# Two steps moved and one PSUM bank exchanged in a one-core transformer block with graph attention

## What is computed

```python
# layer 0, 16 heads of 16
x_mod = rms(x) * (1 + scale_msa) + shift_msa
q, k, v = split(x_mod @ qkv_w)                 # q, k: rms per head, rope
x = x + gate_msa * (softmax(q k^T / 4) v @ proj_w + proj_b)
h = rms(x) * (1 + scale_mlp) + shift_mlp
x = x + gate_mlp * ((silu(h @ w1) * (h @ w3)) @ w2)       # hidden width 704
# layer 1, 16 heads, keys are the first 20 tokens of a sequence
self_feat = concat(x, cond) @ W_self.T + b_self
for d in (0, 1):                               # two directions of the adjacency, 11 labels
    cond_adj, label_bias = A.sum(-1), A @ w_bias + b_bias
    aff = where(cond_adj > 0, (self_feat Wq) (kv Wk)^T / 4, NEG) + label_bias
    output += softmax(aff) kv Wout + bout
return x + relu(output)
```

## Time and profile before

| what | value |
| --- | --- |
| runs | 1407.96, 1402.92, 1408.21 us |
| the profiled execution | 1400.84 us, its span 1398.9 us |
| PE busy | 1334.7 us, 95% of the span |
| weight loads (PEld) busy | 1228.6 us, 88% |
| DVE busy | 1161.8 us, 83% |
| ACT busy | 888.6 us, 64% |
| POOL busy | 719.1 us, 51% |
| mean granted TensorE clock | 0.977 of full |
| time of one pass | 40.97 us (702.16 to 743.13, start of the same step on PE) |

### The profile page before, as it was taken

One profiled execution on the slowest core, in us unless ns is written; L12 is line 12 of the kernel. 1 busy time (PEld: TensorE's weight loads), 2 busy tenths in 40 slices (PEclk: granted clock), 3 DMA queues, 4 the chain that ended last, 5 costly groups with the idle time before them and its releaser, 6 DMA issues. The chain is left out here.

```text
span 1398.9 us, 51521 instructions
## 1 busy us (share of the span) xinstructions
PE 1334.7 (95%) x20276; PEld 1228.6 (88%) x20276; DVE 1161.8 (83%) x2065; ACT 888.6 (64%) x1784; POOL 719.1 (51%) x676
## 2 busy tenths in 40 slices
PE   4589999999999999999999999999999999999986
PEld 3579999999999999999999999999999999999875
DVE  5669888888888888888988888898888888888753
ACT  4557666666766666676666667666667667666542
POOL 0245655555565555456555546555555655555441
PEclk9689999999999999999999999999999999999997
DMA  7001111100011110011111001111100111110100
GB/s 243 29 24 31 46 43 43 43 28 25 33 43 43 43 43 18 33 35 43 43 43 43 15 32 39 43 43 43 43 15 28 43 43 43 43 43 8 30 22 9
DMA packets 49827, 56.19 MB, mean 40 GB/s; under 512 B 4352, under 2 KB 47744, under 8 KB 49792
## 3 DMA queue, kind: packets, MB, share of 16 engines
q1 hardware_dynamic: 48944, 53.86, 12.3%
q10 hardware_dynamic: 848, 1.84, 0.4%
HBM read 47.03 MB, written 8.65 MB: 40 GB/s over the span
## 5 line engine op out<-in xcount | busy, mean ns | idle before, releaser
L1318 POOL TENSOR_TENSOR gl<-gf,gh 128x512 fp32r<-128x512 f32 x96 | 124.2, 1294 | 261.6 <-ACT gh L926 261.6
L486 PE MATMUL psum<-nh,w_lo 128*128 128x256 f32 x704 | 182.7, 289 | 0.0
L486 PE MATMUL psum<-nh,w_hi 128*128 128x256 f32 x704 | 177.7, 284 | 0.0
L1318 POOL TENSOR_TENSOR nl<-xn,nh 128x512 fp32r<-128x512 f32 x64 | 98.3, 1536 | 123.2 <-ACT nh L864 123.2
L486 PEld LDWEIGHTS psum<-nh,w_lo 128*128 128x128 f32 x704 | 133.9, 190 | 0.2 <-issue 0.2
L486 PEld LDWEIGHTS psum<-nh,w_hi 128*128 128x128 f32 x704 | 133.2, 189 | 0.0
L1384 POOL TENSOR_TENSOR e<-e,inv 128x640 f32<-128x640 f32 x64 | 82.0, 1282 | 89.2 <-DVE inv L1274 89.2
L486 PE MATMUL psum<-nl,w_hi 128*128 128x256 f32 x704 | 115.5, 282 | 0.0
L926 ACT ACTIVATE gh<-gf 128x512 fp32r<-128x512 f32 x96 | 60.3, 628 | 61.7 <-DVE gf L1202 60.9
L486 PEld LDWEIGHTS psum<-nl,w_hi 128*128 128x128 f32 x704 | 98.0, 188 | 0.0
L486 PE MATMUL psum<-qkv_lo,nh 128*128 128x512 f32 (+1 forms) x256 | 87.8, 354 | 2.8 <-ACT nh L864 2.8
(11 more groups left out here) (186 smaller groups left out, 4414.0 us busy)
## 6 DMA issues: line engine op xcount, KB each, us to landing
adj<-in_adj SPq DMA_DIRECT2D x32, 440.0 KB, 3.4
x_in<-in_x SPq DMA_DIRECT2D x32, 256.0 KB, 2.7
xn<-in_xT SPq DMA_DIRECT2D x32, 256.0 KB, 3.5
x_res<-in_xT SPq DMA_DIRECT2D x32, 256.0 KB, 3.6
out_T<-y SPq DMA_DIRECT2D x32, 256.0 KB, 2.2
e<-in_adaln ACTq DMA_DIRECT2D x2, 512.0 KB, 5.2
stage<-in_qkv SPq DMA_DIRECT2D x2, 384.0 KB, 5.6
pT<-in_w SPq DMA_DIRECT2D x2, 384.0 KB, 7.1
```

The costliest lines, as they stand in the source:

```text
L486: last = nc.tensor.matmul(out, lhsT, rhs, start=start and i == 0, stop=stop and i == len(terms) - 1)
L1318: return nc.gpsimd.tensor_tensor(out, full, hi.bitcast(F32), ALU.subtract)
```

## The change

ACT's list has `self_split` directly behind `self`, ahead of `norm1_mean` and `keys`. DVE's list has `edges` ahead of the second `mix`; it stood behind `mix1`. The second half of tile 1's transposed probabilities goes to bank 7 and no longer to bank 0, and the waits for free banks follow from that. No instruction is added or taken out.

```diff
-    ..., "probsT": (5, 4, 4, 0), ...
+    ..., "probsT": (5, 4, 4, 7), ...
 DVE:
-        (1, "mlp_up", 1), (2, "mix", 1), (3, "qkv", 0), (3, "qkv", 1), (1, "mlp_up", 2), (0, "mix1", 0),
-        (1, "edges", 0), (3, "rope_scale", 0), (0, "out", 0),
+        (1, "mlp_up", 1), (1, "edges", 0), (2, "mix", 1), (3, "qkv", 0), (3, "qkv", 1), (1, "mlp_up", 2), (0, "mix1", 0),
+        (3, "rope_scale", 0), (0, "out", 0),
 Activation:
-        (2, "heads", 0), (2, "heads", 1), (0, "self", 0), (1, "norm1_mean", 0), (0, "keys", 0), (0, "self_split", 0),
+        (2, "heads", 0), (2, "heads", 1), (0, "self", 0), (0, "self_split", 0), (1, "norm1_mean", 0), (0, "keys", 0),
 PE, qkv, t == 0:
-                    wait_free(pe, m, (v1_kept, -3, 1), (normed[1], -2, 1), (qkT_kept, -1, 1))
+                    wait_free(pe, m, (pT_b, -1, 2))
 PE, score:
-                wait_free(pe, m, (g_done, -2, 3), (pT_b, -1, 2))
+                wait_free(pe, m, (g_done, -2, 3), (shifted_s, -1, 2))
 PE, probs_t, (t, j) == (1, 4):
-                        wait_free(pe, m, (biased1, -2, 4), (shifted_s, 0, 2))
+                        wait_free(pe, m, (v1_kept, -2, 1), (normed[1], -1, 1), (qkT_kept, 0, 1))
 PE, mlp_up, (2, "w3"):
-                        wait_free(pe, m, (pT1_a, -1, 1), (pT_b, 1, 2))
+                        wait_free(pe, m, (pT1_a, -1, 1), (biased1, -1, 4), (shifted_s, 1, 2))
 PE, probs_t1, (t, j) == (0, 0):
-                        wait_free(pe, m, (pT_b, 2, 2), (biased1, 0, 4))
+                        wait_free(pe, m, (biased1, 0, 4))
```

More of the change, by code:

```diff
@@ L72 @@
 BANK = {
-    "xT": 6, "qk": (2, 3), "v": (7, 1), "heads": (7, 5), "probsT": (5, 4, 4, 0), "probsT1": (0, 5, 4, 7),
+    "xT": 6, "qk": (2, 3), "v": (7, 1), "heads": (7, 5), "probsT": (5, 4, 4, 7), "probsT1": (0, 5, 4, 7),
     "mix": (5, 6), "q1": (4, 6), "score": 0, "score1": 0, "mixT": 6, "proj": 2, "norm1": 7, "up": (6, 4, 6),
```

## The result

The changed kernel takes 1390.09 us (median of four, 1388.06 to 1393.36) against 1406.68 us for the kernel before (four runs, 1402.92 to 1408.21). The ratio is 0.9893, 95% interval 0.9870 to 0.9916: faster by 1.1%, 16.6 us between the medians. The prediction said 1391.8, or 16.2 us less.

A forecast was written before the change was run, and what follows sets the result against it. The order of PE's own work was taken to set the time; closing two holes, 10.3 and 6.5 us, less a 0.6 us leftover wait, gave 16.2 off the 1407.96 median: 1391.8 us, range 1385 to 1409.

The forecast's parts named there:

- The bound: PE is busy 40.87 of 41.00 us a pass; two small holes of outside cause cost 0.56 a pass, 16.8 us.
- Self split first: ACT's high part of self_feat earlier: PE's 0.33 wait for POOL's low part goes, 10.3 us, L1086 taking 0.42.
- The first rival: POOL's power holds DVE's L1086, so the 0.33 hole moves to tile 0's transposition; 6.5 to 9.2 us gained; chance 0.20.
- The bank: Fifth transposition of tile 1's probabilities no longer waits for DVE's last bias (L1251): 0.23 x 28 = 6.5 us.
- Edges earlier: DVE's count fits its 1.37 us idle before the second mix; `y` eats the 0.97 freed; costed at zero.
- The sum: -10.3 - 6.5 + 0.6 = -16.2 us, giving 1391.8 us from the median; this forecast's chance 0.52.
- The third rival: POOL's L1368 holds DVE's count, delaying the second mix: PE loses 1.2 us a pass, 34 in all, 1442; chance 0.10 with other losses.
- The second rival: PE's holes return whole at other waits with 0.1 to 0.3 us to spare; time stays at 1408; chance 0.18.

## Why the prediction was right

*The bound.* PE's stream, with two holes of outside cause. Right: with both closed, the pass fell by 0.54 of the 0.56.

*Self split first, 10.3 us.* Right in mechanism, and nearly in size: alone it gives 0.31 a pass, 8.7 us in the loop's 28 passes; the 10.3 counted 31 waits of 0.33. The hole's 0.33 is kept because L1086 comes free, as argued; the version with one scaling moved shows that a later L1086 costs PE what it loses. (L1233 was called a fifth of L1086's size; with 80 of 256 columns it is about a third, which the argument doesn't need.) The first rival rested on POOL's power holding L1086. The trace after has just that overlap in the pass shown, and L1086 at 415 ns in the median of all passes. The Trainium skill, page "SBUF — State Buffer", section "Who interferes with whom", has the two exclude each other for the whole instruction; for the full-size operations that nearly holds here (L1086 before the change ends 0.29 behind POOL's operation, L1131's pair 0.61, `y` 0.54; but with an overlap of 0.21 L1086 lost only 0.07), for the power on 128x2 it does not.

*The bank, 6.5 us.* Right in the loop: 0.21 a pass alone, 5.9 us over 28 passes, nothing in its place. Of the new wait of `qkv` it said "I cost these at nothing", with 3 us to spare in the steady pass. That holds in the loop, but ahead of it PE waits 1.1 us once.

*Edges earlier, zero.* Right on both sides: the count fitted into the idle time with 0.16 to spare (0.1 said), and `y` ate the whole gain behind it (1.58 us, "about 1.6" said).

*The sum.* 16.2 us said. The loop's share is 28 x 0.54 = 15.1, less 1.5 once for the bank and the count in the first passes; the medians differ by 16.6, with an interval of about 12 to 18. That the forecast hit within 0.4 is luck; that it lies in the interval is not. The two profiled executions differ by 11.2 (1400.84 to 1389.65): taking the forecast from the median, not from the one profiled execution, was right by more than the reason given, since that execution had been spared a break of PE that most have.

*The third rival's price* is the step that was wrong. It said "From the mix to the MLP's last low part there is no slack", because POOL ends at 714.44 and PE loads at 714.50. That the two follow each other closely didn't mean that DVE's row is what sets them. Before the low part stands ACT's high part, which waits for ACT's own square root and its table as well as for DVE, and on DVE stood an L1131 that was waiting for POOL. The chain that binds first is another, through the first L1125 and ACT's copies to L806, and it had 0.69 to spare. The mix can come 0.74 late for 0.06. A count held for 1.8 us, as the rival had it, would, as an estimate from the count made three times (1.7 late, 1.04 a pass over the changed kernel), have cost 0.5 to 0.6 a pass over the kernel before, 14 to 17 us in 28 passes where 34 were said. The rival's condition did not occur: the count beside L1368 took 1060 to 1066 ns in all passes.

*The second rival*, holes that return whole elsewhere, did not occur either. Its margins were as thin as it said (0.16 at the mix), but each moved with PE.

## What to carry to other kernels

When PE is busy for 95% of the time, list the waits of its weight loads that recur in every pass; each with an outside cause is a gain of its own size, provided the next wait on the same chain is worked out to the hundredth. Before a late instruction is priced, follow every chain that leaves it, through the other engines too, to PE's next load, and take the one with the least to spare. Rows that take longer than elsewhere may be waiting for another engine already, and that wait is slack, but only for what stands behind them. Work out the first and last passes by themselves: a bank that is free 3 us early in the steady pass cost 1.1 us in an unrolled one. And a saving on DVE can be lost where it lets an operation with two SBUF inputs start inside a POOL operation: here `y` took back 0.94 of 0.97.

## What was not expected of the hardware

- The power on 128x2 did not hold DVE up: it takes 0.70 us and L1086 beside it 0.41, its shortest time. A scaling of 128x512 that overlaps L1086's start by 0.21 us adds 0.07.
- Delaying DVE by 0.97 us a pass cost 0.06, the next 0.97 cost 0.98.
- PE breaks off for 1.5 to 2.3 us in the unrolled second pass, always ahead of the same weight load, 15 from the end of `score1`, in 11 of 14 profiles, of the kernel before as well. The trace shows no releaser, and the cause is open.
